# Second attention of a two-block model on one core: scores of a head pair on 32 rows of their own, issued ahead of the transposes, with the row maxima subtracted on Pool

## What is computed

```python
HEADS = 16
def _mha(q, k, v):
    qh, kh, vh = (a.reshape(B, 64, 16, 16).transpose(0, 2, 1, 3) for a in (q, k, v))
    scores = jnp.einsum('bhqd,bhkd->bhqk', qh, kh) / math.sqrt(16)
    scores = jnp.where(causal, scores, -10000.0)
    attn = jax.nn.softmax(scores, axis=-1)
    return jnp.einsum('bhqk,bhkd->bhqd', attn, vh)
x = x + tanh(g_xattn[0]) * cross_attention(_layernorm(x), ctx)
x = x + tanh(g_ffn[0]) * experts_0(_layernorm(x))
x = x + tanh(g_xattn[1]) * _mha(_layernorm(x), ctx, ctx)
x = x + tanh(g_ffn[1]) * experts_1(_layernorm(x))
```

## Time and profile before

| what | value |
|---|---|
| median of 3 runs | 745.74 us |
| lowest and highest run | 741.71 and 748.94 us |
| the profiled execution, own time | 742.05 us |
| its span, first to last instruction | 740.3 us |
| PE busy | 599.4 us (81%) |
| DVE busy | 491.1 us (66%) |
| ACT busy | 335.4 us (45%) |
| POOL busy | 228.8 us (31%) |
| mean granted clock of TensorE | 0.878 |

### The profile page before, as it was taken

The page is one execution under the profiler, slowest core; times in us unless marked ns, Lnnn a source line. Parts: engine busy times, 40 slices in busy tenths (PEclk is TensorE's granted clock), DMA queues, the critical chain, the costliest instruction groups (busy, mean ns, idle before and its releaser), DMA issues. The chain is left out here.

```text
span 740.3 us, 11571 instructions
## 1 busy us (share of the span) xinstructions
PE 599.4 (81%) x3938; PEld 480.7 (65%) x3938; DVE 491.1 (66%) x843; ACT 335.4 (45%) x572; POOL 228.8 (31%) x221
## 2 busy tenths in 40 slices
PE   4799836018999999996258847987899999999996
PEld 1389724018999999996224436765677676776775
DVE  2345583508778778750569978865678778788764
ACT  2233204017677686681047724445444553544531
POOL 3366121540000000002657824221245355354300
PEclk9799865558999999998559978986999999999998
DMA  8310000447576776704302002020202202202001
GB/s 275 138 37 17 14 0 0 163 151 272 196 254 204 241 246 201 267 30 153 116 23 64 28 11 74 0 81 0 78 3 80 77 4 79 79 0 81 1 0 58
DMA packets 49035, 70.33 MB, mean 95 GB/s; under 512 B 6391, under 2 KB 40926, under 8 KB 47966
## 3 DMA queue, kind: packets, MB, share of 16 engines
q1 hardware_dynamic: 46734, 64.49, 26.4%
q0 software_dynamic: 1568, 4.20, 1.7%
q10 hardware_dynamic: 688, 1.05, 0.5%
HBM read 58.71 MB, written 11.03 MB: 94 GB/s over the span
## 5 line engine op out<-in xcount | busy, mean ns | idle before, releaser
L850 PE MATMUL bank<-xhi,wlo 128*128 128x256 f32 x240 | 68.4, 285 | 4.0 <-issue 4.0
L1470 POOL TENSOR_TENSOR wlo<-raw,whi 128x1408 fp32r<-128x1408 f32 (+1 forms) x16 | 46.2, 2906 | 74.0 <-ACT whi L1475 74.0
L850 PE MATMUL bank<-xhi,whi 128*128 128x256 f32 x240 | 68.3, 284 | 0.0
L850 PE MATMUL bank<-xlo,whi 128*128 128x256 f32 x240 | 68.2, 284 | 0.0
L868 PE MATMUL bank<-whi,hlo 128*128 128x256 f32 x240 | 67.7, 282 | 0.0
L868 PE MATMUL bank<-wlo,hhi 128*128 128x256 f32 x240 | 66.5, 277 | 0.0
L868 PE MATMUL bank<-whi,hhi 128*128 128x256 f32 x240 | 66.5, 277 | 0.0
L1127 POOL DMA_INDIRECT ceg<-moe_const,crow x1 | 0.9, 918 | 187.5 <-DMA moe_const<-yb 187.5
L1939 PE MATMUL bank<-xhi,wlo 128*128 128x512 f32 x128 | 55.6, 434 | 2.4 <-DVE xlo L2041 2.4
L1071 DVE TENSOR_TENSOR hlo<-ga,hhi 128x512 fp32r<-128x512 f32 x60 | 40.1, 689 | 19.4 <-ACT hhi L918 19.4
L230 PE MATMUL bank<-ident,hn 128*128 128x128 f32 x64 | 16.5, 430 | 44.2 <-DVE hn L221 44.2
(11 more groups left out here) (323 smaller groups left out, 1693.1 us busy)
## 6 DMA issues: line engine op xcount, KB each, us to landing
raw<-w_in SPq DMA_DIRECT2D x16, 1024.0 KB, 5.7
rawb<-w_in SPq DMA_DIRECT2D x14, 1024.0 KB, 5.9
raw<-wf_in SPq DMA_DIRECT2D x8, 1088.0 KB
moe_rows<-zrow SPq DMA_DIRECT2D x1, 3840.0 KB, 14.7
xs<-moe_rows SPq DMA_DIRECT2D x15, 256.0 KB, 6.1
moe_out<-yb SPq DMA_DIRECT2D x15, 256.0 KB
scb<-sc_in SPq DMA_DIRECT2D x16, 160.0 KB
cv<-ctx_in SPq DMA_DIRECT2D x32, 64.0 KB, 2.1
```

The costliest lines, as they stand in the source:

```text
L850: last = nc.tensor.matmul(psum[b][:, half:half + ST], w[:, s, at:at + P], a[:, s, k, :], start=(n == 0), stop=(n == 3 * KT - 1))
L1470: nc.gpsimd.tensor_tensor(wlo[:, s, a:b], raw[:, a:b], whi[:, s, a:b].bitcast(F32), ALU.subtract).then_inc(to, 1)
```

## The change

The changes are in the block ahead, in the attention block and, for one constant, in the first block.

- A mask `pmask` is made once from `hmask` by two small additions on POOL. Its last two columns pick the even and the odd heads.
- `kx` now holds the keys twice instead of eight times: once with the odd heads zero, once with the even heads zero. A row group of 32 partitions (NR = 4 of them) holds just two heads. The scores of these two come from a matmul over the 32 partitions alone, with 128 columns.
- So a tile has 16 score matmuls (2 halves, 2 sequences, 4 row groups) of 32 rows, 64 weight columns and 128 columns, where it had four of 128 rows, 64 weight columns and 512 columns. Each row group writes to its own bank; all tiles use the same four banks, half filled. The mask matmuls are four of 256 columns, where they were two of 512.
- The queries are taken from `qT` directly; the copies `qs` and their ACT instructions go.
- Both halves of scores(n+1) are issued ahead of transposes(n).
- DVE takes the lower bound in four instructions of 256 numbers each (one for each bank) and one row maximum for both halves. POOL subtracts the maxima, in two instructions of 512 numbers for each tile, in its list ahead of the splitting of keys for the tile after next.
- PE's steps are written out instead of a loop. DVE's and ACT's loops stay.

```diff
@@ helpers
-                nc.gpsimd.tensor_tensor(kx[:, j, k, :, :], rows(keys, HT), each(hmask[:, :], S), ALU.mult
+                nc.gpsimd.tensor_tensor(kx[:, j, k, :, :], rows(keys, mask.shape[1]), each(mask, S), ALU.mult
                                         ).then_inc(kx_ready, 1)
@@ first block, POOL
+                        g.wait()
+                        g(nc.gpsimd.tensor_tensor(pmask[:, 0:4], hmask[:, 0:4], hmask[:, 4:8], ALU.add))
+                        g.wait()
+                        g(nc.gpsimd.tensor_tensor(pmask[:, 4:6], pmask[:, 0:2], pmask[:, 2:4], ALU.add))
@@ block ahead
-            kx = buf("kx6", [P, XC, KT, HT, S], F32, s5)
+            kx = buf("kx6", [P, XC, KT, 2, S], F32, s5)
...
-                        split_keys(pool, ctxT, kx, kx_ready, j, j)
+                        split_keys(pool, ctxT, kx, kx_ready, j, j, pmask[:, 4:6])
@@ attention block, POOL
-                        with pool.Fori(1, NI) as it:
-                            for j in range(XC):
-
-                                pool.wait_ge(s_done, XC * it + 2 * (j // 2) + 2)
-                                split_keys(pool, ctxT, kx, kx_ready, XC * it + j, j)
+                        for n in range(NT):
+                            s = n % XR
+                            for k in range(KT):
+                                part = sm[:, s, k, :, :]
+                                pool.wait_ge(mx_ready, n + 1)
+                                nc.gpsimd.tensor_tensor(part, part, each(mx[:, s, k, :], S), ALU.subtract
+                                                        ).then_inc(sub_ready, 1)
+                            if n + XR < NT:
+                                pool.wait_ge(s_done, 2 * n + 2 + XC)
+                                for h in range(2):
+                                    split_keys(pool, ctxT, kx, kx_ready, 2 * (n + XR) + h, 2 * s + h, pmask[:, 4:6])
@@ attention block, PE
+                        def scores(tile):
                             n, s = tile
+                            pe.wait_ge(kx_ready, KT * (2 * n + 2))
+                            pe.wait_ge(s_read, NR * (n + 1))
+                            for r in range(NR):
+                                nc.tensor.matmul(psum[r][:, 0:2 * KT * S], ident_r[:, :], rows(far_r[:, :], 2 * KT),
+                                                 start=True, stop=False)
+                            for k in range(KT):
+                                for h in range(2):
+                                    own = slice(h * S, (h + 1) * S)
+                                    for r in range(NR):
+                                        dims = slice(32 * r, 32 * r + 32)
+                                        last = nc.tensor.matmul(psum[r][own, 2 * k * S:2 * (k + 1) * S],
+                                                                qT[dims, k, (2 * n + h) * S:(2 * n + h + 1) * S],
+                                                                kx[dims, 2 * s + h, k, :, :].rearrange(
+                                                                    "p h s -> p (h s)"), start=False, stop=(k == KT - 1))
+                            last.then_inc(s_done, 2)
...
-                            for k in range(1, KT):
-                                if nxt is not None:
-                                    scores(nxt, k)
...
-                        over_tiles(pe, step)
+                        scores((0, 0))
+                        over_tiles(pe, step, unrolled=True)
@@ attention block, DVE
                             dve.wait_ge(p_turned, KT * (n + 1))
+                            dve.wait_ge(s_done, 2 * n + 2 + XC)
+                            for r in range(NR):
+                                part = sm[:, s, :, 2 * r:2 * r + 2, :]
+                                nc.vector.tensor_tensor(
+                                    part, psum[r][:, 0:2 * KT * S].rearrange("p (k h s) -> p k h s", k=KT, h=2),
+                                    lo_b[:, :].unsqueeze(1).unsqueeze(1).broadcast_to([P, KT, 2, S]), ALU.max
+                                    ).then_inc(s_read, 1)
+                            dve.wait_ge(s_read, NR * (n + 2))
+                            nc.vector.tensor_reduce(mx[:, s, :, :].rearrange("p k h -> p (k h)"),
+                                                    sm[:, s, :, :, :].rearrange("p k h s -> p (k h) s"), AX.X, ALU.max
+                                                    ).then_inc(mx_ready, 1)
@@ attention block, ACT
-                        def queries(tile):
...
-                                act.wait_ge(mask_step, 2 * (KT * n + k) + 2)
+                                act.wait_ge(sub_ready, KT * n + k + 1)
```

More of the change, by code:

```diff
@@ L62 @@
 XC, XR = 4, 2
+NR = P // 32
 class Steps:
@@ L113, in build @@
         tg = buf("tg", [P, 4])
+        pmask = buf("pmask", [P, 6])
         stats = buf("stats", [P, NT, 6])
@@ L151, in slot_rows, with split_keys, over_tiles @@
             return table[CAP * i:CAP * i + ST, :].rearrange("(t p) d -> p t d", p=P)
[L153 removed]
+        def split_keys(pool, keysT, kx, kx_ready, b, j, mask):
             for k in range(KT):
                 keys = keysT[:, k, ds(b * S, S)]
[L157 removed]
+                nc.gpsimd.tensor_tensor(kx[:, j, k, :, :], rows(keys, mask.shape[1]), each(mask, S), ALU.mult
                                         ).then_inc(kx_ready, 1)
[L160 removed]
+        def over_tiles(engine, step, unrolled=False):
             def body(it, last):
@@ L166, in body @@
                     step(*(None if last and s + d >= XR else after[d] for d in range(3)))
-            with engine.Fori(0, NT // XR - 1) as it:
-                body(it, False)
+            if unrolled:
+                for it in range(NT // XR - 1):
+                    body(it, False)
+            else:
+                with engine.Fori(0, NT // XR - 1) as it:
+                    body(it, False)
             body(NT // XR - 1, True)
@@ L1249, in _ @@
                         pe.sem_inc(pv_done, XC)
-                        def scores(tile, k):
+                        def scores(tile):
                             n, s = tile
[L1253 to L1265, removed]
+                            pe.wait_ge(kx_ready, KT * (2 * n + 2))
[13 more added lines that the diff above has]
+                            last.then_inc(s_done, 2)
@@ L1267, in step @@
                         def step(tile, nxt, _):
                             if nxt is not None:
-                                scores(nxt, 0)
+                                scores(nxt)
                             n, s = tile
@@ L1292, in step @@
                                         last.then_inc(pv_done, 1)
-                        for k in range(KT):
-                            scores((0, 0), k)
-                        over_tiles(pe, step)
+                        scores((0, 0))
+                        over_tiles(pe, step, unrolled=True)
                     @block.vector
                     def _(dve):
-                        dve.sem_inc(s_read, KT * XR)
+                        dve.sem_inc(s_read, NR)
                         dve.sem_inc(o_added, XR)
@@ L1350, in _ @@
                         act.sem_inc(vx_ready, 2 * XC)
-                        def queries(tile):
-                            n, s = tile
-                            for h in range(2):
-                                j = 2 * s + h
-                                act.wait_ge(s_done, 2 * n + 2)
-                                apart(act, turns)
-                                nc.scalar.activation(qs[:, j, :, :], qT[:, :, ds((2 * n + h) * S, S)], ACT.Copy
-                                                     ).then_inc(qs_ready, 1)
                         def values(tile):
@@ L1392, in step @@
                             if after is not None:
-                                queries(after)
                                 values(after)
```

24 lines of the change are left out of this document (5 added, 19 removed).

## The result

The changed kernel took 751.83 us (median of 8 runs, 746.45 to 769.89) beside 745.31 (8 runs, 741.71 to 748.94) of the kernel before: 1.0077 times, interval 1.0041 to 1.0113. The longest run, 769.89, was in a slower state and is left out of this ratio; the seven others lie at 746.45 to 752.83. The forecast was 740.4 with a range up to 750: wrong in size and in direction. What happened is what rival 4 describes, the low clock through the block, to which I gave 0.09.

What follows compares the result with a forecast made beforehand. Bound: two about equally long rings, PE with ACT (period 5.87 us) and a nearly full DVE. Gains 1.7 + 0.7 + 2.9 = 5.3 took 742.05 to 736.8; that execution lay 3.7 below the median, hence 740.4, range 734 to 750.

Steps and rivals of the forecast that it cites:

- rival 4: Attention block: clock stays low throughout because PE has less to do; period 7.4, 5.2 more, 750.9 us; chance 0.09.
- Start: Start of the attention block: clock rises one tile later, first period about 7.0 instead of 5.87; 0.7 us gained.
- T6: Start of tile 6's transposes in the attention block: forecast 43.7 us behind the block's start, before 44.35.
- Subtraction: POOL, attention block: each subtraction of 512 numbers priced at 1.04 to 1.24 us, taken as 1.1, two a tile.
- splitting: POOL, attention block: each splitting of 128 numbers between 0.26 and 0.74 us, taken as 0.5, four a tile.
- rival 2: Attention block: POOL becomes the bound, 5.94 us a tile; only 1.6 less, 744.1 us; chance 0.12.
- Scores in one piece: PE, attention block: a tile's scores take 1.9 us together, bounds 1.3 and 4.6, hidden up to 2.5 beside ACT.
- Rival 3: PE, attention block: row groups don't run side by side, scores 4.6, period 7.6; 8.9 more, 754.6 us; chance 0.08.
- The ring: PE and ACT's repeating cycle per attention tile: PV starts 0.34 us sooner, so the period falls from 5.87 to 5.5.
- Block ahead: Block before the attention: shorter POOL splittings let `hn` finish sooner; 1.7 us less, between 1.0 and 2.2.
- End of the block: Attention block's end: `wlo` comes last and the last addition waits; T6 + 11.4 instead of 14.29, 2.9 us gained.
- Rival 1: Attention block: clock rises at once and splittings are short; 7.6 less, 738.1 us; chance 0.21.

Runs made afterwards that it cites:

- e3: The changed kernel plus unread filler matmuls on PE, at the end of the block ahead and in each attention step; 745.03 us, 0.9986 of the kernel before.
- e2: The changed kernel, unedited, measured and profiled a second time; 750.28 us, 1.0101 of the kernel before.
- e5: The changed kernel with the second half of the scores put back between transposes and PV, row groups kept; 760.77 us, ratio 1.0213.
- e4: The changed kernel with scores over 128 rows and 512 columns again, new order kept, key splitting left out behind the first two tiles; 749.21 us, ratio 1.0050.
- e6: As e3, with more unread filler matmuls ahead of the block, behind the first scores and in the first step; 740.64 us, ratio 0.9946.
- e1: The kernel before, unedited, measured and profiled a second time; 745.18 us, ratio 1.0017.
- e7: As e6, with POOL's two long `wlo` products moved from the end of its list to places where it waits; 736.33 us, ratio 0.9890.

## Why the prediction was wrong, point by point

**The step that failed** is "Start ... I expect the clock to rise one tile later", with the reason given against rival 4, that PE would be busy nearly all of the period at the low clock. In three of four profiles the clock never rose in the block. The reason had two faults. PE was busy for 5.1 to 5.2 of 6, not for nearly all of it as in the 6.41 of 6.50 of the earlier trace rows: the scores need 2.3 at that clock and not 3.0, and PE still waits 0.69 for the copies and 0.2 for the exponentials in each tile. And PE's busy share doesn't tell the granted clock by itself: the clock rose behind 6.00 of 6 in e3, but also behind 5.12 of 6 in the first profile of the changed kernel, and it didn't rise behind 5.81 of 6 in e2.

**What is shown of the cause.** Four runs carry it: e5 (row groups, old order: 0.50), e4 (new order, no row groups: 1.00), and e3 and e6 (row groups and fillers: 1.00 once it has risen, or from the start; e6 is 1.5% faster than e2 by the ratios 0.9946 and 1.0101). What it is in the row groups' matmuls that costs the clock, no run separates: their 32 rows, their smaller size, or only that they are done sooner and leave PE less to do (4.13 of 6 at clock 0.99, where e4 had 5.1 to 5.2 at 1.00). The fillers have 128 rows and also fill the time, so they don't tell these apart either.

**Its price.** (7.02 - 5.45) x 6 periods = 9.4; measured between e2 and e6 at T6: 51.8 - 42.1 = 9.7. The forecast had 43.7 there. Rival 4 had 7.4 for the period. Its ring was right and one term too long: scores of 3.0 behind PV are 2.3 at 1.2 GHz (404.60 to 406.91) and stay hidden behind ACT's 2.4.

**Rival 4's sum came out near the truth for a wrong part.** It gave 750.9; the median is 751.83. But by its own terms the typical run (e2 against e1) has T6 7.8 later, the end 2.6 shorter and the block ahead 2.2 shorter: +3.0, where it said +5.2. The rest of the measured 6.5 lies outside the two blocks, where no rival had anything: in the means of the table +3.6 behind and +0.9 in front. The agreement of 750.9 and 751.83 is luck.

**Terms that held.** Four of them are seen in e2's groups, 393 to 436 us, which answer to the earlier trace rows:

```profile
L1248 POOL TENSOR_TENSOR sm<-sm,mx 128x512 f32<-128x512 f32 x12 | 12.3, 1042 | 20.2 <-DVE mx L1333 20.2
...
L1328 DVE TENSOR_TENSOR sm<-bank,lo_b 128x256 f32<-128x256 f32 x23 | 8.2, 417 | 5.5 <-PE bank L1278 5.5
L159 POOL TENSOR_TENSOR kx<-ctxT,pmask 128x128 f32<-128x128 f32 x20 | 8.1, 435 | 0.0
...
L1333 DVE TENSOR_REDUCE mx<-sm 128x16 f32<-128x1024 f32 x5 | 6.1, 1221 | 0.2
```

- Subtraction 1.04 (I took 1.1), splitting 0.44 (0.5), maximum 0.42 (0.42), reduction 1.22 (1.25). POOL is idle for 20.2 of these 43, waiting for maxima, and in e6 the period is 5.45 with ACT waiting for PV: rival 2 is out.
- Scores in one piece: 1.36 at 2.4 GHz, where I took 1.9; the 32 records take 0.69, where one after the other would be 3.8. Rival 3 is out. The Trainium skill (TensorE: Matmul & The Clock Gate, "Measured speedup vs the span model") gives 3.07 times for four row tiles with 512 columns. The trace agrees that they run side by side: 3.8, which is my estimate, against 0.69 is 5.5 times, with 128 columns and with column halves side by side as well.
- The ring with the clock: 5.45 in e6, forecast 5.5.
- Block ahead: 2.2 less, forecast 1.7 and 2.2 as its upper bound. It answers to the earlier trace rows with `hn` 3.08 for 5.58, where I had named 4 as the sign:

```profile
375.80 3.08 DVE L227 TENSOR_SCALAR hn<-x,mv,rstd 128x256 f32<-128x256 f32 x8
...
377.05 1.69 POOL L159 TENSOR_TENSOR kx<-ctxT,pmask 128x128 f32<-128x128 f32 x4
```

- End of the block: `wlo` became last, as forecast, and the additions stall on it. The first profile, answering to the earlier trace rows:

```profile
431.38 1.18 PE L1292 MATMUL bank<-ident,sm 128*128 128x128 f32 x8 [1.14 <-ACT sm L1384]
...
435.17 5.91 POOL L1257 TENSOR_TENSOR wlo<-raw,whi 128x1280 fp32r<-128x1280 f32 x2
435.20 3.15 DVE L1351 TENSOR_TENSOR x<-x,o 128x256 f32<-128x256 f32 x1
...
439.76 1.61 DVE L1351 TENSOR_TENSOR x<-x,o 128x256 f32<-128x256 f32 x1
```

From T6 to the end of the last addition there are 9.99, where the forecast had 11.4 and the kernel before 14.29; this stretch had the clock at 1.00 in this profile, and in e2, at 0.50, it is 10.95. The rule of the Trainium skill that I weighed (SBUF — State Buffer, "Who interferes with whom") held at both additions: 3.15 and 1.61 beside the products, 0.43 and 0.42 without them (e7).

**Rival 1** (clock up at once, 738.1) is what e6 made true by hand, at 740.64.

**What stays open.** The blocks behind are unchanged code, run 3.6 longer in the mean of four profiles each, and the two sets don't overlap. Their mean granted clock is 0.92 to 0.93 in either kernel. Of the 3.6, 2.2 come with the one DVE instruction that stands behind POOL's product, as shown above; that holds for e6 and e7 too, whose attention block has the clock, so it doesn't come from the low clock there. What makes POOL come first, and the remaining 1.4, stay open; e7 is as short behind the block (300.1) as the kernel before. Part of the 0.9 in front is a stage that takes 219.9 to 220.2 in two profiles of the kernel before and 223.9 to 224.7 in the two others and in every profile of the other kernels; whether that is chance, no run here tells. Behind and in front together that is 4.5 in the means of the table, more than the 1.4 of the two blocks of the change.

## What to carry to other kernels

Matmuls packed onto row groups finish sooner, but a stage that leans on them can lose TensorE's higher clock for all its other matmuls: here the shorter and earlier scores gave 0.42 in each tile (5.87 to 5.45, with fillers), and without fillers the clock took 1.57. Before such a change, look at the granted clock in the windows of that stage, and don't take PE's busy share as a sign that it will hold, least of all a share at the low clock: the same kernel had 5.1 of 6 at 0.50 and 4.1 of 6 at 0.99. If the clock falls, a few unread matmuls in the gaps may bring it back. And when a long POOL product becomes the last thing in a block, put it where POOL waits.

## What the runs showed of the hardware that I had not expected

- The same busy share beside either clock: mostly 5.1 to 5.2 of 6 at granted clock 0.50 for over 40 us (e2), 5.1 to 5.2 of 6 at 1.00 (e4), 4.8 of 6 at 1.00 in the kernel before.
- The same kernel can go either way: in the first profile of the changed kernel the clock was 0.99 in one window and then fell back to 0.58 and 0.50, with no change in the work, while in the three other profiles it stayed at 0.50.
- A lead of 0.10 decides: `h1lo` on DVE takes 0.68 when it starts 0.10 ahead of POOL's product, and 3.71 when it starts 0.24 behind it.
- Extra work made the kernel faster: e6 runs 139 more matmuls than the changed kernel, and its ratio to the kernel before is 0.9946 where e2's is 1.0101.
